# Norms of an eight-stage transformer program computed in two parts, the first part ahead of the stage before

## The reference, cut to what matters

```python
x = x + _L0_xattn_ref(_layernorm(x, axis=-1), ctx_1024, ...)   # strided cross attention
x = x + _L0_attn_ref(_layernorm(x, axis=-1), ...)              # distances as scores
x = x + _L0_ffn_ref(_layernorm(x, axis=-1), ...)               # 8 experts, top 2, and a shared one
x = x + _L1_xattn_ref(_layernorm(x, axis=-1), ctx_1024, ...)   # decoder block
x = x + _L1_attn_ref(_layernorm(x, axis=-1), ...)              # differential attention block
x = x + _L1_ffn_ref(_layernorm(x, axis=-1), ...)               # product-key memory
```

```python
y = layernorm(y + sa, g1, beta1)                 # _L1_xattn_ref: after causal attention
y = layernorm(y + ca, g2, beta2)                 # after cross attention
h = jax.nn.relu(jnp.einsum('bsd,df->bsf', y, w1) + b1)
y = layernorm(y + jnp.einsum('bsf,fd->bsd', h, w2) + b2, g3, beta3)
...
h = _layernorm(x, ln1_g, ln1_b)                  # _L1_attn_ref
conn = skip + _diff_attn(h, ...)
h2 = _layernorm(conn, ln2_g, ln2_b)
return conn + jax.nn.relu(h2 @ W1.T + b1) @ W2.T + b2
```

## Time and profile before

| | |
|---|---|
| median of 3 runs | 3369.82 us (3367.12 to 3372.61) |
| the profiled execution, its own time | 3393.56 us |
| its span, first to last instruction | 3391.8 us |
| mean granted TensorE clock | 0.861 of full speed |
| PE busy | 2537.7 us (75%) |
| DVE busy | 1788.1 us (53%) |
| ACT busy | 912.2 us (27%) |
| POOL busy | 850.6 us (25%) |

### The profile page before, as it was taken

How to read it: one execution, slowest core, us unless ns; L and a number is a source line. 1 busy time by engine, 2 the same in 40 slices (tenths; PEclk the granted TensorE clock), 3 DMA queues, 4 the chain that set the end, 5 groups by cost and what they waited for, 6 DMA issues and landing times. The chain is left out here.

```text
span 3391.8 us, 47607 instructions
## 1 busy us (share of the span) xinstructions
PE 2537.7 (75%) x16384; PEld 1818.6 (54%) x16384; DVE 1788.1 (53%) x7054; ACT 912.2 (27%) x2012; POOL 850.6 (25%) x1020
## 2 busy tenths in 40 slices
PE   5796889578994889858895789938898488957544
PEld 3584567344772558535673557725585356733321
DVE  2313455745647438464557456374384645572447
ACT  1212242123321233222421233212332224212210
POOL 0102114312223213221143122232132311432042
PEclk8698899779996899969997799968999799976666
DMA  6075145141533226131451415322261414512100
GB/s 235 31 262 195 38 143 196 43 157 58 191 133 110 88 85 232 60 144 38 143 196 42 164 54 187 132 93 107 78 230 66 147 39 143 196 43 101 25 0 7
DMA packets 215096, 392.64 MB, mean 116 GB/s; under 512 B 83728, under 2 KB 167952, under 8 KB 189616
## 3 DMA queue, kind: packets, MB, share of 16 engines
q1 hardware_dynamic: 208688, 372.49, 32.0%
q0 software_dynamic: 6144, 16.79, 1.5%
HBM read 350.55 MB, written 38.67 MB: 115 GB/s over the span
## 5 line engine op out<-in xcount | busy, mean ns | idle before, releaser
L841 PE MATMUL ps<-xbT,stream 128*128 128x128 f32 x2560 | 316.0, 277 | 12.8 <-DMA stream<-in_experts 8.3
L841 PEld LDWEIGHTS ps<-xbT,stream 128*128 128x128 f32 x2560 | 303.2, 192 | 32.2 <-DMA stream<-in_experts 15.8
L302 POOL TENSOR_TENSOR hTB<-pb,sbuf 128x2048 f32<-128x2048 f32 x32 | 152.2, 4769 | 416.9 <-DVE pb L1703 416.9
L652 PE MATMUL ps<-cmat,aTB 128*128 128x512 f32 x256 | 137.8, 688 | 92.4 <-DVE sbuf L1788 81.3
L473 POOL TENSOR_TENSOR rstdA<-veA,mhalf 128x4 f32<-128x4 f32 x24 | 24.4, 1018 | 700.4 <-DVE veA L1332 700.4
L473 POOL TENSOR_TENSOR rstdB<-veB,mhalf 128x4 f32<-128x4 f32 x48 | 48.9, 1018 | 494.3 <-DVE veB L1332 494.3
L1062 PE MATMUL ps<-ident,work 128*50 128x128 f32 x32 | 12.0, 375 | 210.2 <-POOL work L617 194.1
L841 PE MATMUL ps<-xbT,ctxA 128*128 128x128 f32 x1280 | 158.2, 277 | 4.5 <-DMA ctxA<-in_experts 4.4
L841 PEld LDWEIGHTS ps<-xbT,ctxA 128*128 128x128 f32 x1280 | 150.8, 192 | 14.3 <-DMA ctxA<-in_experts 8.9
L644 PE MATMUL ps<-ident,xnB 128*128 128x128 f32 x256 | 55.5, 338 | 135.8 <-DVE xnB L1339 103.1
L854 PE MATMUL ps<-stream,hTA 128*128 128x256 f32 x640 | 151.9, 380 | 0.6 <-ACT yb L1190 0.6
(11 more groups left out here) (283 smaller groups left out, 5988.6 us busy)
## 6 DMA issues: line engine op xcount, KB each, us to landing
stream<-in_experts SPq DMA_DIRECT2D x88, 1024.0 KB, 5.2
stream<-in_experts SPq DMA_DIRECT2D x88, 512.0 KB, 6.2
ctxA<-in_experts SPq DMA_DIRECT2D x40, 1024.0 KB
work<-in_ctxT SPq DMA_DIRECT2D x32, 1028.0 KB, 7.2
hTB<-in_ctxN SPq DMA_DIRECT2D x32, 1024.0 KB, 7.0
down<-in_experts SPq DMA_DIRECT2D x40, 512.0 KB
ctxA<-in_ctxT SPq DMA_DIRECT2D x16, 1024.0 KB, 9.2
stream<-in_ctxT SPq DMA_DIRECT2D x16, 1024.0 KB, 11.4
```

Of the source, the lines that this page charges most:

```text
L302: return e.tensor_tensor(out.rearrange("p (a d h) -> p a d h", a=8, d=16), a.unsqueeze(2).broadcast_to([P, 8, 16, 16]), vals[:, t, :].rear ...
L652: ins = mm(out, aT[:, k, t * P:(t + 1) * P], wt[:, k, cols], start=k == 0, stop=k == KT - 1)
L841: ins = mm(ps[:, 2 * (b % 2) + u, f * P:(f + 1) * P], wu[:, u, k, f * P:(f + 1) * P], xbT[:, b % 2, k, :], start=k == 0, stop=k == KT - 1)
```

## The change

Seven norms, all but y0, are made in two parts: tiles 0 to 2 and tile 3 for y1, y2, h2 and n5, tiles 0 and 1 and tiles 2 and 3 for y3, z and h1. Each part has its own epsilon add, its own root on POOL and its own scaling, all of it on DVE; the share of ACT and the product made for it are gone. The first part's root, scaling, transposes and evictions stand in the last slots of the stage ahead, DVE's scaling of part 0 for instance before the last tile's result of that stage. The slots of back become fewer, and ORDER is a new string (186 slots in place of 199).

```diff
+        PARTS = dict.fromkeys(("y1", "y2", "h2", "n5"), (range(T - 1), range(T - 1, T)))
+        PARTS.update(dict.fromkeys(("y3", "z", "h1"), (range(HALF), range(HALF, T))))
+        TURNED = dict.fromkeys(("y1", "y2", "h1", "h2"), ((5, 0), (6, 0)) * 2)
+        TURNED["n5"] = ((6, 0), (7, 0)) * 2
...
+                        def rstd(tag, p):
+                            pool.wait_ge(vec_done, V[tag, "var", p])
+                            nc.gpsimd.tensor_tensor(rstdB[:, span(tag, p)], veB[:, span(tag, p)], mhalf[:, 0:len(PARTS[tag][p])],
+                                                    ALU.pow).then_inc(pool_done, O.step(tag, "rstd", p))
...
+                    def turn(tag, t, src, place):
+                        bank, c = place
+                        wait_scaled(pe, tag, t)
+                        if t >= 2:
+                            pe.wait_ge(act_done, A[tag, "T", t - 2])
+                        for k in range(KT):
+                            ins = tr(ps[:, bank, c + k * P:c + (k + 1) * P], src[:, t, k * P:(k + 1) * P], ident)
+                        ins.then_inc(pe_done, PE.step(tag, "T", t))
...
+                            if i == T + 1:
+                                for t in PARTS["h2"][0]:
+                                    turn("h2", t, hh, TURNED["h2"][t])
+                            yield
+                        for t in PARTS["h2"][1]:
+                            turn("h2", t, hh, TURNED["h2"][t])
...
                         def sim(t):
-                            pe.wait_ge(act_done, A["n5", "T", T - 1])
+                            pe.wait_ge(act_done, A["n5", "T", max(t, T - 2)])
...
-                        yield from norm("n5", xnB, (5, 6), lambda: sim(0))
+                        pe.wait_ge(vec_done, V["h2", "f2", T - 1])
+                        sim(0)
+                        for t in PARTS["n5"][1]:
+                            turn("n5", t, xnB, TURNED["n5"][t])
...
+                    def variance(tag, p):
+                        for t in PARTS[tag][p]:
+                            v.wait_ge(vec_done, V[tag, "st", t])
+                            vv.bn_aggr(mvB[:, t, :], stB[:, t, :]).then_inc(vec_done, V.step())
+                        own_steps()
+                        vv.tensor_scalar(veB[:, span(tag, p)], mvB[:, span(tag, p), 1], EPS, None, ALU.add).then_inc(
+                            vec_done, V.step(tag, "var", p))
+
+                    def scaled_part(tag, p, src, dst):
+                        v.wait_ge(pool_done, O[tag, "rstd", p])
+                        for t in PARTS[tag][p]:
+                            vv.tensor_scalar(dst[:, t, :], src[:, t, :], mvB[:, t, 0:1], rstdB[:, t:t + 1], ALU.subtract,
+                                             ALU.mult).then_inc(vec_done, V.step(tag, t))
...
+                            if i == T + 1:
+                                scaled_part("y2", 0, xnB, xnB)
                             if i >= 2:
                                 t = i - 2
...
                                 stats("y2", xnB, smallB, t)
-                            yield
+                            if i >= T:
+                                variance("y2", i - T)
+                            yield
...
+                        def more(p):
+                            scaled_part("y3", p, xnB, xnB)
...
+                            variance("z", p)
+                        def first_of_layer(p):
+                            scaled_part("z", p, xB, xnB)
...
+                            variance("h1", p)
...
+                        def under_y2(i):
+                            if i == 2:
+                                variance("y3", 0)
+                            if i == 3:
+                                more(0)
+                            if i == 4:
+                                variance("y3", 1)
+                                first_of_layer(0)
+                        yield from ffn("y2", "y2b", xnB, under_y2)
+                        more(1)
+                        scaled_part("h1", 0, xnB, hh)
+                        yield
+                        first_of_layer(1)
+                        yield
+                        scaled_part("h1", 1, xnB, hh)
```

More of the change, by code:

```diff
@@ L426, in back @@
                             "p (t d) -> p t d", t=T)).then_inc(ctxl_in, 16)
-                        for _ in range(3 + T + 2 + 3):
+                        for _ in range(3 + T + 2 + 1):
                             yield
@@ L436, in back @@
                             yield
-                        for _ in range(3 + 8 + T + 1 + 8):
+                        for _ in range(1 + 8 + T + 1 + 3):
                             yield
@@ L576, in back @@
                             add("xc", t, xB[:, t], xB[:, t], xnB[:, t])
-                        for _ in range(8 + T + 1):
+                        for _ in range(1 + 8 + 3):
                             yield
-                        yield from norm("n5", veB, rstdB)
+                        rstd("n5", 0)
+                        yield
+                        rstd("n5", 1)
+                        yield
+                        yield
                         for i in range(T + 2):
@@ L1644, in ffn @@
                             for i in range(T + 1):
+                                if i == T and tag == "h2":
+                                    then(i)
                                 if i >= 1:
```

195 lines of the change are left out of this document (128 added, 67 removed).

## The result

| | before | after |
|---|---|---|
| median of the runs | 3370.0 us (3367.12 to 3372.61, 4 runs) | 3247.56 us (3240.4 to 3249.26, 4 runs) |
| the profiled execution's span | 3391.8 us | 3245.3 us |
| mean granted TensorE clock | 0.861 | 0.874 |
| first group | 291.7 us | 286.2 us |
| middle group, mean of seven | 394.9 us | 377.6 us |

The ratio is 0.9638 (95% interval 0.9625 to 0.9650): 122 us faster. Forecast were 86, in a range from 46 to 108. So the sign was right, the size wrong and outside the range.

A forecast was written before the change was run, and what follows sets the result against it. No engine bounds a whole group; back's chain of dependent steps does, with front filling its holes. Gains of 10.4 us in each of seven middle groups (72.8) and 12.7 in the last, 85.5 in all, gave 3284 us, range 3262 to 3324.

The forecast's parts named there:

- So no engine is the bound for a whole group ... back is a chain of dependent steps: Middle group: front fills the holes of back's chain, so shortening the chain shortens the group unless front takes the time back.
- h2, 3.9: Norm ahead of the second feed-forward: the feed-forward starts 3.9 us earlier per middle group, 3.9 behind `conn` instead of 7.8.
- n5, 4.1: Norm between second feed-forward and last stage's scores: scores start 1.6 us behind the feed-forward's end, not 5.65; gain 4.1.
- y3, z, h1, 2.2: Norms from the first feed-forward's last result to the qkv products: gain 2.2 us per middle group.
- y1, 0, and y2, 0.7: Norms ahead of cross attention and the first feed-forward: gain 0 (bounds -0.5 and +0.8) and 0.7 us per middle group.
- The last stage, -0.5: From the search on: two more expert products on DVE, less a wait of about 0.9; cost 0.5 us per middle group.
- Cross attention, and qkv to the scores, nothing: Stages of a middle group that the change does not edit: no gain forecast, 0.
- Rival C: Second feed-forward's first half: PE's clock falls, each middle group loses 2.1 of h2's 3.9; 3299 us, chance 0.11.
- Rival B: Front's dense queues ahead of the second feed-forward: y1, y2 and h1 gain nothing there; 3305 us, chance 0.20.
- D: End of the group: the gather becomes the end and the kernel gets slower, 3379 us; chance 0.04.
- E: Front truly bounds a middle group by queue order, so just the last group gains; 3364 us, chance 0.03.
- the gather came where it was forecast: Last stage: gather starts about 37 us behind the search and ends at 47; the later sum stays covered.

The follow-up runs named there:

- second pair of profiles: Unchanged copies of the kernel before and of the changed kernel, run and profiled again; the middle group's change summed to -14.3 us, against -17.4 in the first pair.
- order_y2: Changed kernel with fourteen of front's 68 slots (causal attention's tail to first feed-forward) back at the old kernel's places, one or two slots away; ratio 0.9773.
- after_oldorder: Changed kernel, norms in parts, with front's slots where the kernel before has them; ratio 0.9920 to the kernel before.
- before_neworder: Kernel before, norms whole, with front's slots moved to where the changed kernel has them; ratio 1.0135 to the kernel before.
- whole_h2: Changed kernel with the norm h2 alone made whole again; ratio 0.9714, 28 us more than the changed kernel.
- warm_h2: Changed kernel with ten spare products on PE in the gap of h2, five ahead of the fourth tile's transposes and five behind; ratio 0.9640.
- h2gap_warm_last: Changed kernel with two front slots moved from the last stage to ahead of the second feed-forward, plus eleven spare PE products in the last stage; ratio 0.9692.
- halves: Changed kernel with y1, y2 and h2 split into two and two tiles instead of three and one; ratio 0.9643.
- warm_start: Changed kernel with 24 spare products on PE at the start of each group of back, ahead of norm y0; ratio 0.9707.
- warm_both: Changed kernel with 24 spare PE products at each group's start and ten more in the gap of h2; ratio 0.9657.

## Why the forecast was right in sign and wrong in size

In the second pair of profiles a middle group gained 3.9 more than the forecast's 10.4: h1 2.4, cross attention 1.7, last stage 1.6, y1 1.3, qkv 0.9 and y2 0.3 more, against the clock of the second feed-forward 2.1, the first feed-forward 0.8, the attention 0.8, h2 0.4 and n5 0.2. By the step:

- **"So no engine is the bound for a whole group ... back is a chain of dependent steps"**: right. In a middle group DVE has 8 us and POOL 3 us more work than before, and the group is 17 us shorter (14 in the second pair).
- **h2, 3.9**: 3.5 by the trace, and 28 us in the experiment against 30. Right, with two errors that cancel: the root 0.46 shorter than counted, the small steps between the engines longer.
- **n5, 4.1**: right for this change; the gap shrank by 3.9, and the scores were at full clock before it too (3.70). In the new order the experiment prices it at 65, not 32.6, of which 45 or so can be seen in the trace: the term took a wait of PE as a wait alone; behind a wait of 3.1 the scores lose another 2.4 to the clock, and these DVE waits for.
- **y3, z, h1, 2.2**: the step that failed most, 4.5. I had let one root wait of 1.1 go and kept h1's, and counted front's product of 0.69 besides; the product stands in that wait, so one of the two was counted twice (0.9). The add of the last result came 0.45 late and not 1.0 (0.55). The roots of two columns took 0.69 to 0.80 (0.3). Some 0.6 are not accounted for. The evictions, 1.6 and 0.4, were right.
- **y1, 0, and y2, 0.7**: too small; measured 1.3 to 1.4 and 1.0 to 1.4, and 19 and 34 us by experiment. The step that failed is that the forecast had kept front's queue as it was read before, and did not price the new string at all. The new order takes front's waiting operations from in front of the second scaling; `order_y2` shows what one of them costs.
- **The last stage, -0.5**: it gained 1.1 to 2.2. The wait of the second tile fell from 2.37 to 1.68 as expected. Not expected: DVE in before also stalls for 1.6 to 2.4 us in all in small pieces, in each of the 14 middle groups of its two profiles, at the end of POOL's issues of the gather, such as these (the last issue ends at 1834.99):

```profile
1835.10 0.09 DVE L1812 MATCH_VALUE_LOAD hTB<-sbuf 128x8 f32 x1 [0.53 <-DVE hTB L1812]
...
1836.52 0.20 DVE L1812 MATCH_REPLACE8 hTB<-sbuf 128x50 f32<-128x50 f32 x1 [1.15 <-issue]
```

  In the changed kernel it is 0 to 0.6, and its gather ends beside another part of the search. It goes with the order and not with the parts: 1.6 to 2.4 also in `after_oldorder`, whose gather starts 30 behind the search as in before (29), and at most 1.0 in all other kernels, where it starts 35 to 38 behind, in `before_neworder` with whole norms 0.4 to 0.7. That the place of the gather is the cause is only argued; no run moved it alone.
- **Cross attention, and qkv to the scores, nothing**: they gained 1.7 to 2.5, and 0.9. The first is the clock, above. The second is only in part: from the start of the qkv products to the scores a group of before takes 27.3 to 27.5 at 0.93 and 27.8 to 28.4 at 0.90 to 0.92, one of after 26.5 to 26.7 at 0.94 and 27.6 to 27.9 at 0.90. So some 0.6 of the 0.9 is there at about the same clock, and what that is stays open.
  The forecast had no term for stretches that the change does not touch.
- **Rival C**, "if that lowers the clock, each middle group loses 2.1": came true (+2.0 and +2.1 in the mean), with a chance of 0.11. That it fits to the tenth is luck: of the seven groups of either profile one keeps the 14.0 of before, and the others lose 1.5 to 3.1. My argument against it, that the gap gets shorter, was wrong: what PE does in the gap counted. In `whole_h2` the gap is 2.6 longer and the half as slow, 16.9 for 16.7 from its first product to the second half. The Trainium skill (TensorE: Matmul & The Clock Gate, "What's actually happening") says that full clock is released by activity and that the idle state is the half clock; `warm_h2` and `h2gap_warm_last` agree, 14.0 for 16.6 and 3.67 for 6.25 by products that compute nothing. I had set it up as a case of its own; it was one term of the sum, and the same clock gave as much back in the cross attention.
- **Rival B**, front takes it back: not in this order; it is what happens in the old one, where the parts are worth 27 us. **D** and **E** did not occur: the gather came where it was forecast.
- **The range** failed because all its ends were made of the same terms. None held a gain from the new order of the slots, none the clock in stretches that are not edited, and none the roots' length by columns (at most 23 us by the estimate above; I had written that roots of one and three columns would take about the same).

Of `warm_h2`, `halves`, `warm_start` and `warm_both`, which might have been faster than the changed kernel, none is.

## What to carry to other kernels

When engines are fed by one written order, a split of a step and the order around it are one change: price the split with every queue as it will stand, and look in each for another stream's operation that waits ahead of the new step. A wait of TensorE on the path can cost its length and then nearly as much again, since the next products run in part at half clock (here 2.4 and 2.7 us behind waits of 3.1 and 2.9). Independent work, useful or not, put into the wait gives that stretch back its clock, and the same work moved elsewhere can warm another stage; whether the total follows has to be measured, as it did in `h2gap_warm_last` and did not in `warm_h2`. And read the duration of the shape you will have, not of the shape you have: where no row shows it, the range has to reach to a gain as well.

## What was not expected of the hardware

- A root (`pow`) on POOL over 128 partitions takes 0.55 us for one column, 0.73 for two, 0.89 for three and 1.02 for four, about 0.16 for each column beyond the first.
- Eight matmuls of 512 columns with cmat: 3.60 to 3.67 us at full clock, 6.03 to 6.25, at 0.58 to 0.61, when PE had waited 2.9 to 3.1 us shortly before. A stage of some 498 matmuls with waits on other engines: 52.2 us at 0.95, 56.5 at 0.86.
- The same kernel can be granted another clock in the same stage of different groups of one execution (`warm_h2`: 0.95 in two, 0.86 in two others), worth 4.7 us a group. What decides it stays open.
- DVE's stalls of 0.2 to 1.15 us ahead of `MATCH_REPLACE8` and `MATCH_VALUE_LOAD`, within 1.6 us on either side of the end of POOL's last issue of eight indirect transfers, above; the cause stays open.
